# Attention and MLP block on one core: another slot table for the units of two shared PSUM banks, pivot rows copied in their own slot, and scale and shift of the transposed input on ScalarE

## The reference

```python
h = _modulate(_layernorm(x), shift_msa, scale_msa)        # x * (1 + scale) + shift
qkv = h @ W_qkv + b_qkv                                   # 16 heads of 36
scores = jnp.einsum('blhd,bmhd->bhlm', q * scale, k)
attn = jax.nn.softmax(scores, axis=-1)
o = jnp.einsum('bhlm,bmhd->blhd', attn, v).reshape(b, l, c)
x = x + gate_msa * (o @ W_proj + b_proj)
```

## Time and profile before

| what | us |
|---|---|
| median of 3 runs (lowest, highest) | 2611.95 (2607.66, 2615.72) |
| the profiled execution's own time | 2613.1 |
| its span, first to last instruction | 2611.3 |
| PE busy in the span | 2348.9 (90%) |
| DVE busy | 1424.7 (55%) |
| ACT busy | 1100.5 (42%) |
| POOL busy | 807.3 (31%) |
| stretch 130 to 1300 us (attention): PE busy | 1059.1 of 1170.0 |

### The profile page before, as it was taken

The page is one execution under the profiler, slowest core; times in us unless marked ns, Lnnn a source line. Parts: engine busy times, 40 slices in busy tenths (PEclk is TensorE's granted clock), DMA queues, the critical chain, the costliest instruction groups (busy, mean ns, idle before and its releaser), DMA issues. The chain is left out here.

```text
span 2611.3 us, 43520 instructions
## 1 busy us (share of the span) xinstructions
PE 2348.9 (90%) x15081; PEld 2023.5 (77%) x15081; DVE 1424.7 (55%) x2994; ACT 1100.5 (42%) x2362; POOL 807.3 (31%) x1587
## 2 busy tenths in 40 slices
PE   6598989989899898998997269999999999999998
PEld 1466767767677576675775259999999999999998
DVE  3577687777877777777674562333333333333332
ACT  2265555565565565655554122222222222222221
POOL 2044343443544445444444661111111111111110
PEclk9799999999999899999998589999999999999998
DMA  7122222222222222222221340101110101111100
GB/s 233 38 77 71 64 78 74 85 74 64 81 73 81 78 61 79 75 73 87 59 66 49 93 127 12 37 31 37 31 37 31 37 31 37 31 37 31 37 26 28
DMA packets 100228, 159.95 MB, mean 61 GB/s; under 512 B 23680, under 2 KB 44256, under 8 KB 100000
## 3 DMA queue, kind: packets, MB, share of 16 engines
q1 hardware_dynamic: 86752, 110.35, 14.7%
q0 software_dynamic: 12240, 46.60, 5.7%
q10 hardware_dynamic: 1024, 0.26, 0.0%
HBM read 80.10 MB, written 20.16 MB: 38 GB/s over the span
## 5 line engine op out<-in xcount | busy, mean ns | idle before, releaser
L1644 PE MATMUL bank<-h2T,w 128*128 128x256 f32 x4032 | 530.6, 283 | 2.8 <-DVE h2T L1584 2.8
L1644 PEld LDWEIGHTS bank<-h2T,w 128*128 128x128 f32 x4032 | 508.2, 191 | 3.3 <-DVE h2T L1584 3.3
L1553 DVE TENSOR_TENSOR glo<-bank,ghi 128x256 fp32r<-128x256 f32 x288 | 122.1, 424 | 681.3 <-ACT bank L1520 681.3
L1657 PE MATMUL bank<-w,ghi 128*128 128x288 f32 x2304 | 477.3, 298 | 0.0
L1519 ACT ACTIVATE ghi<-bank,b 128x256 fp32r<-128x256 f32 x288 | 136.9, 475 | 680.6 <-PE bank L1644 680.5
L869 DVE TENSOR_TENSOR plo<-pf,phi 128x512 fp32r<-128x512 f32 x512 | 372.4, 727 | 80.0 <-ACT pf L739 77.5
L862 DVE TENSOR_REDUCE negm<-bank 128x1 f32<-128x512 f32 x512 | 347.7, 679 | 77.6 <-PE bank L1018 75.3
L1657 PEld LDWEIGHTS bank<-w,ghi 128*128 128x128 f32 x2304 | 367.1, 189 | 2.1
L1657 PE MATMUL bank<-w,glo 128*128 128x288 f32 x1152 | 340.8, 296 | 0.0
L736 ACT ACTIVATE phi<-bank 128x512 fp32r<-128x512 f32 x512 | 307.3, 600 | 25.8 <-PE bank L1046 11.9
L739 ACT ACTIVATE pf<-bank 128x512 f32<-128x512 f32 x512 | 309.3, 604 | 0.2
(11 more groups left out here) (222 smaller groups left out, 3289.3 us busy)
## 6 DMA issues: line engine op xcount, KB each, us to landing
qs<-qkhi SPq DMA_DIRECT2D x192, 72.0 KB
ks<-qkhi SPq DMA_DIRECT2D x192, 72.0 KB
wst<-w_fc POOLq DMA_DIRECT2D x34, 288.0 KB, 3.1
xln<-x POOLq DMA_DIRECT2D x32, 288.0 KB, 3.5
xln<-x POOLq DMA_DIRECT2D x8, 1152.0 KB, 6.2
x_d<-xln POOLq DMA_DIRECT2D x32, 288.0 KB, 2.5
xa<-x_d SPq DMA_DIRECT2D x32, 288.0 KB, 2.8
xs<-x_d SPq DMA_DIRECT2D x16, 576.0 KB, 3.8
```

The costliest lines, as they stand in the source:

```text
L1644: mm = pe.matmul(F[ft % 2][:, 0:CH], w1[0:rows, w, ft * PAR:(ft + 1) * PAR], h[0:rows, a, :], start=(i == 0), stop=(i == len(FULL_PASSES) ...
L1657: mm = pe.matmul(Y[2 * tt + half][:, 0:HALF], g[ft % 2][:, span], w2[:, ft, w, half * HALF:(half + 1) * HALF], start=(ft == 0 and i == 0), ...
```

## The change

It does four things. `FIRST_SLOT`, `IN_ONE_SLOT` and the slots of statistics, loads and normalisation are other tables. The copy of a pivot row and of an `rv` result (`take_row`, `take_rotation`) is made by DVE in the unit's own slot instead of the next, SP issues the next `wrot` load in the unit's slot instead of two slots later, and `el` h stands in slot 4h+1 for every h, its POOL step in slot 4h+2. `modulate` on DVE is gone: ACT computes `scale * x + shift` twice from the transposed bank, once into `hT` as the high part and once in place in the bank, from which DVE takes the low part as before. The wait for the last low part of `hT`, which tile 0 of `qk` had, goes to whichever unit of the next batch comes first, now `v` 0 0.

```diff
 EARLY_QK = 3
-FIRST_SLOT = [(0, ("v", 1, 0)), (2, ("v", 1, 1)), (4, ("qk", 3)), (6, ("v", 1, 2)), (7, ("tr", 0)), (9, ("p", 0, 0)),
...
+FIRST_SLOT = [(1, ("v", 1, 0)), (3, ("qk", 3)), (6, ("v", 1, 1)), (7, ("tr", 0)), (9, ("qk", 4)), (11, ("p", 0, 0)),
...
-BROADCAST_SLOT = {h: TT * h + 1 for h in range(HEADS)} | {0: 2, 10: 40, 11: 46}
+BROADCAST_SLOT = {h: TT * h + 1 for h in range(HEADS)}
...
-STEP_SLOT = {(38 if _h == 9 else TT * _h + 3): _h for _h in range(HEADS)}
+STEP_SLOT = {BROADCAST_SLOT[_h] + 1: _h for _h in range(HEADS)}
...
                 def hT_his(it, f):
-                    act.wait_ge(modulated, (it + 1) * (KT + 1) + f + 1)
-                    bank = G[g_bank(it, ("ln", f))]
-                    if f < KT:
-                        act.activation(hT[:, f, :], bank[:, :], ACT.Copy).then_inc(hT_hi, 1)
-                    else:
-                        act.activation(hT[0:REM, 2 * KT, :], bank[0:REM, :], ACT.Copy).then_inc(hT_hi, 1)
-                        act.activation(hT[REM:PAR, 2 * KT, :], bank[0:REM, :], ACT.Copy).then_inc(hT_hi, 1)
+                    rows = PAR if f < KT else REM
+                    bank = G[g_bank(it, ("ln", f))][0:rows, :]
+                    grow, add = (adaT[0:rows, j, f, bass.ds(it + 1, 1)] for j in (1, 0))
+                    act.wait_ge(g_full, g_use(it, ("ln", f)) + 1)
+                    for dst in (hT[:, f, :],) if f < KT else (hT[0:REM, 2 * KT, :], hT[REM:PAR, 2 * KT, :]):
+                        act.activation(dst, bank, ACT.Identity, bias=add, scale=grow).then_inc(hT_hi, 1)
+                    act.activation(bank, bank, ACT.Identity, bias=add, scale=grow).then_inc(hT_hi, 1)
...
-                    for u in units(b, ENDS_AT[n]):
-                        if u[0] == "ln":
-                            modulate(b, u[1])
...
+                    for u in units(b, ENDS_AT[n]):
                         if u[0] == "el":
                             take_row(b, u[1], phase)
```

More of the change, by code:

```diff
@@ L81 @@
 EARLY_QK = 3
-FIRST_SLOT = [(0, ("v", 1, 0)), (2, ("v", 1, 1)), (4, ("qk", 3)), (6, ("v", 1, 2)), (7, ("tr", 0)), (9, ("p", 0, 0)),
[5 rows of a table removed]
+FIRST_SLOT = [(1, ("v", 1, 0)), (3, ("qk", 3)), (6, ("v", 1, 1)), (7, ("tr", 0)), (9, ("qk", 4)), (11, ("p", 0, 0)),
[6 rows of a table added]
 RV = 4
-BROADCAST_SLOT = {h: TT * h + 1 for h in range(HEADS)} | {0: 2, 10: 40, 11: 46}
+BROADCAST_SLOT = {h: TT * h + 1 for h in range(HEADS)}
 FIRST_SLOT = sorted(FIRST_SLOT + [(_n, ("el", _h)) for _h, _n in BROADCAST_SLOT.items()], key=lambda at: (at[0], at[1][0] != "el"))
-IN_ONE_SLOT = [("v", 1, 2), ("v", 1, 3), ("p", 0, 1), ("p", 1, 0), ("p", 2, 0), ("p", 2, 1)]
+IN_ONE_SLOT = [("v", 1, 2), ("v", 0, 0), ("v", 0, 1), ("v", 0, 3), ("p", 0, 0), ("p", 0, 1), ("p", 1, 0), ("p", 2, 0), ("p", 2, 1), ("p", 3, 1)]
 TR_SLOT = [_n for _n, _u in FIRST_SLOT if _u[0] == "tr"]
+FIRST_OF_H = [u for _, u in FIRST_SLOT if u[0] == "qk" and u[1] < EARLY_QK or u[0] == "v" and u[1] == 0][0]
 assert all(_n % TT == TT - 1 for _n in TR_SLOT)
 MAX_LEAD = 10
[L95 to L98, removed]
+LOAD_AT = {18: 0, 23: 1, 27: 2, 32: 3}
+STAT_AT = {21: 0, 26: 1, 30: 2, 35: 3}
+INVERT_AT = {31: (0, 3), 36: (3, 4)}
+LN_NORM_AT = {32: 0, 34: 1, 38: 2, 39: 3}
 RESIDUAL_SLOT = 48
 EARLY = 5
-EARLY_SLOT = 28
+EARLY_SLOT = 38
 ACT_LAG, DVE_LAG = 1, 1
-STEP_SLOT = {(38 if _h == 9 else TT * _h + 3): _h for _h in range(HEADS)}
+STEP_SLOT = {BROADCAST_SLOT[_h] + 1: _h for _h in range(HEADS)}
 def shift(unit):
@@ L458, in build @@
         CONSTANTS = RING + 5
-        modulated, hT_hi = sem("modulated"), sem("hT_hi")
+        hT_hi = sem("hT_hi")
         g_full, g_free = sem("g_full"), sem("g_free")
@@ L526, in slot @@
                 def slot(b, n):
-                    for _, i in [u for u in units(b, ENDS_AT.get(n - 2, [])) if u[0] == "rv"]:
+                    for _, i in [u for u in units(b, ENDS_AT[n]) if u[0] == "rv"]:
                         if not isinstance(b, int) or RV * b + i + 1 < RV * BATCH:
@@ L800, in _ @@
                 dve.sem_inc(o_read, 1)
[L802 to L808, removed]
                 def hT_los(it, f):
                     rows = PAR if f < KT else REM
-                    dve.wait_ge(hT_hi, (KT + 2) * (it + 1) + (f + 1 if f < KT else KT + 2))
+                    dve.wait_ge(hT_hi, (2 * KT + 3) * (it + 1) + (2 * f + 2 if f < KT else 2 * KT + 3))
                     part = hT[0:rows, KT + f if f < KT else A_PARTS - 1, :]
@@ L938, in v_tile @@
                     if part == 0:
+                        if u == FIRST_OF_H:
+                            pe.wait_ge(g_free, g_use(it, ("ln", KT)) + 3)
                         pe.wait_ge(g_free, g_use(it, u) + 1)
@@ L948, in qk_tile @@
                     if part == 0:
-                        if t == 0:
+                        if u == FIRST_OF_H:
                             pe.wait_ge(g_free, g_use(it, ("ln", KT)) + 3)
```

## The result

| | before | after |
|---|---|---|
| median of 4 runs | 2612.8 us | 2699.85 us (2696.22 to 2708.07) |
| ratio | 1 | 1.0334, 95% interval 1.0314 to 1.0355 |
| profiled execution (its span) | 2613.1 us (2611.3) | 2696.22 us (2694.4) |
| first to last `values` matmul | 1282.4 us | 1360.4 us |
| one batch, batches 1 to 6 | 164.7 us | 175.0 us |

The changed kernel is 87 us slower, 3.3%. The forecast was slower by 41 us, at 2654, with 2692 as the upper end: the sign is right, the size half of what came. The third stage takes 1205 us in both. All of the loss lies ahead of it: of the 83 us between the two profiled executions, 78 lie in the 512 slots and 5 before the first of them.

The account below looks back on a forecast made before the run. PE was taken to set the attention's pace, busy 1059 of 1170 us. From 2613.1 us, -48 without transfers and +90 for late tiles gave 2655, or 2654 as median; range 2605 to 2692, slower at 0.80.

Parts of the forecast that it names:

- part f: Slots 38 and 54: PE waits about 4.4 us for transfers of late qk tiles, with slower matmuls behind: +90 us.
- the second price: Slots 38 and 54: matmuls behind each transfer wait run at 1.2 GHz, 1.5 us more per wait, 23 us in all.
- The term of 1.5 us: Ahead of the first batch: v 0 0 before qk 0 delays the first tile by 14 matmuls, +1.5 us.
- Part a: Slot 40: pivot row 10 gets four slots after row 9, so PE's wait for POOL shrinks: -30 us.
- Part c: The ln slots: scale and shift on ACT instead of DVE make seven slots together about 1 us shorter: -7 us.
- Parts a to e: All effects except the late tiles' transfers, called the sum without transfers: -48 us.
- part b: Shared banks: 18 units no longer start while the bank they need is being read out: -37 us.
- Part d: Slots 34, 35 and 39: qk 7 and 8 fill short slots where PE waits for DVE's low part: -11 us.
- Part e: Slots behind each tr: the head's transposes wait for DVE to split the bank, without unit work: +37 us.
- The lower clock costs more: Rival: full slots behind the 4.4 us waits cost 2.8 us each, 2675 to 2690; the forecast's upper end.
- The rows arrive in time: Rival at slots 38 and 54: transfers land before PE needs them, so faster, 2565 us; chance 0.14.
- ACT becomes the bound: Rival: ACT sets the pace in the whole stage; chance 0.02, within the forecast's upper end.

Follow-up runs that it names:

- e1_both: The changed kernel with both late tiles moved earlier, qk 7 to slots 31 and 32 and qk 0 to 49 and 50: 2620.05 us, 1.0028.
- e10_row10: The kernel before with scale and shift moved to ACT and pivot row 10 broadcast in slot 41 instead of 40: 2589.25 us, 0.9906.
- e4_before_act: The kernel before, with its own slot table, and only scale and shift moved from DVE to ACT: 2607.60 us, 0.9978.
- e7_dve_mod: The changed kernel with scale and shift moved back to DVE, everything else as changed: 2715.08 us, 1.0393.
- e9_fill: The changed kernel with qk 7 and qk 0 moved earlier, and v 1 2 put in empty slot 24: 2617.69 us, 1.001.
- e6_busy: The changed kernel with unread extra matmuls at slots 9, 17, 21 and 25, written to the next unit's shared bank: 2700.76 us, 1.0336.
- the best table: The kernel before with scale and shift on ACT, pivot row 10 in slot 41, and p 2 0 in slot 22: 2582.98 us, 0.9886.

## Why the prediction was half right

| | forecast | runs | from |
|---|---|---|---|
| late tiles (f) | +90 | +80 | changed kernel less `e1_both` |
| the rest (a to e) | -48 | +6 | `e1_both` less before |
| sum | +42 | +87 | |

The sign came out right because part f, which held, is larger than the rest.

**Part f held.** Place, chain and size: 2.94 and 8.82 us behind V(35) for 3.0 and 9.0. The waits are 3.9 us at slot 38 and 3.1 at slot 54 instead of 4.4, since PE gets there later than at V(35) + 4.6; in the sum that is 8 x 3.9 + 7 x 3.1 = 53 us for 66. The rest of the 80, 27 us, is the second price, put at 23; by the busy times of the changed kernel and `e1_both` it is 31. The first slot starts 5 us later in the profiled execution (V(0) at 129.2 for 123.8); the other kernels lie between 123.9 and 130.0, so that alone can't be told from their spread. The wait ahead of batch 0's first score matmul can: 6.2 us in the changed kernel and in the three runs that keep `v` 0 0 first and add nothing there, 4.3 in the three with tile 0 first, 2.7 on the old table. The term of 1.5 us is right for the order of the two units (1.9); the table adds as much again.

**Part a held.** Slots 40 and 41 take 4.23 us together where they took 7.81, 3.6 a batch for nearly 4. On the old table `e10_row10` gave 18 us for row 10 alone; its slot 40 fell from 4.53 to 1.78 us, 22 us in eight batches, of which slots 41 and 43 took some back.

**Part c held on the old table,** by `e4_before_act` (-6 for -7); on the new one `e7_dve_mod` makes it 15. The duration failed, 0.78 for 0.69 us. The estimate by the figure of the Trainium skill, which made part c about zero, had the duration right and the gain wrong.

**Parts a to e together failed: -48 forecast, +6 measured.** Their account closes from the waits of PE in the two traces. These are the lines of `e1_both`, 130 to 1400 us:

```profile
PE bank L1028 <- ACT pf L741: 33.5, 50, 1.5
PE bank L1052 <- DVE aT L827: 30.3, 28, 2.0
PE bank L1039 <- DVE plo L863: 27.6, 53, 1.0
PE bank L1039 <- ACT ots L748: 10.3, 47, 0.3
PE bank L1012 <- DMA ks<-qklo: 6.4, 10, 2.1
PE bank L1012 <- issue: 3.2, 1, 3.2
```

| standing of PE, 130 to 1400 us | before | `e1_both` | change | forecast |
|---|---|---|---|---|
| pivot rows (a) | 27.9 | 0.6 | -27 | -28 of the -30 |
| banks (b) | 24.0 | 0 | -24 | -24 of the -37 |
| ACT's and DVE's lag: `pf`, `plo`, `hT` (c, d) | 61 | 61 | 0 | -18 |
| transposes behind `tr` (e) | 3.8 | 30.3 | +26 | +37 |
| ACT's copy of the head's output (`ots`) | 0.2 | 10.3 | +10 | none |
| transfers (slots 2 and 54, and one of 3.2 us) | 2.0 | 9.6 | +8 | none |

With 3 us of small ones gone, this is -10 us, as the two stretches say (-9), where the waits in the forecast make -33. The other 15 us of the -48 (2 of part a, 13 of part b) were to come from shorter slots behind the waits, and PE's busy time rose by 12 instead. That is 24 + 27 us, and 3 more stand before the first slot in the profiled executions: together the 54 us between -48 and +6.

**So the steps that failed are these.** *In parts a and b the clock was counted only as a gain.* The waits went as priced, and the low clock of slots 36, 40 to 42 and 48 went too, but `e1_both` has it in slots 9, 17, 45, 46 and 49, and PE is busy 12 us longer in place of 15 shorter. *Part d's and part c's standing was not won*: 61 us in both. Slots 34 and 35 take 1.85 and 2.29 us in `e1_both`, before 1.64 and 2.43. *The emptied slots were priced at nothing*: in slots 8, 16, 20, 24, 40 and 52, which now have no unit, PE works 1.1 to 1.2 us and then stands 0.2 us until ACT has copied the head's output; that is all 10 us of the `ots` line. Slots 5, 29, 42 and 61 of the changed kernel are as short (1.4 us), but PE works all through them. *Part e was sized as a wait and given no clock term*, as the next paragraph shows. Its own four terms also make 5.7 us a batch and not the 5.3 of the text, which is 40 us and not 37.

**Part e held as a wait and failed as a price.** The transposes wait for DVE at slots 9, 17, 21 and 25 of every batch, 28 times, 30.1 us for 3.8 before: +26 for the +37. But behind the wait of 1.66 us at slot 17 the fullest slot of the table runs at 1.2 GHz, and slots 16 and 17 take 8.03 us for 5.33, with less unit work in them than before. The same at slot 49. The timeline of PE in the changed kernel, first a `v` unit at full speed in batch 4, then `v` 0 0 behind its wait in batch 5:

```profile
972.18 2.07 PE L935 MATMUL bank<-wv,hT 128*128 128x288 f32 x14
...
1121.64 0.49 PE L1028 MATMUL bank<-qs,ks 109*128 109x512 f32 x1 [1.45 <-ACT pf L741]
...
1125.22 3.71 PE L935 MATMUL bank<-wv,hT 128*128 128x288 f32 x14
```

It takes 3.71 us for 2.07. Slot 49 takes 5.50 us, before 3.01. Neither slot had a clock term; I asked about the clock only behind waits of over 3 us.

The rows of before could have told this. The prediction takes the 4.14 us of the earlier trace rows for a slot behind a long wait. It is slot 36 of batch 5, the wait ahead of it is of 1.04 us, and its seven matmuls take 2.84 us:

```profile
1026.31 2.84 PE L953 MATMUL bank<-hT,wqk 128*128 128x512 f32 x7
```

The same slot is slow in three batches of the eight (4.1 us) and fast in five (2.6 us), behind waits of the same length. So a low clock behind a short wait was there before the change, in some batches and not in others, and the earlier trace rows show the opposite case, 2.68 us followed by a matmul at 0.50. The Trainium skill (TensorE: Matmul & The Clock Gate, "Why this matters for your kernels") warns of gaps between bursts of matmuls. The trace agrees that gaps go with the low clock, but the gaps here, 1.04 to 1.66 us, are well under the one that the page warns of; the measurement decides.

**The rivals.** "The lower clock costs more" is part of what came, but not where it put it: it had the excess behind the waits of part f, at 2675 to 2690, and it came behind those of part e and of the `ln` slots. "The rows arrive in time" is out by the timeline of slots 38 and 54, "ACT becomes the bound" by 779 of 1364 us. The range ended at 2692 because parts b, d and e were given no bound of their own on the other side; with b and d at nothing, it would have ended at 2740.

**Why the table has these gaps** I can only argue from the code. The count by which a unit knows that its bank is free rises in the order of the table, and a pivot row is now read in its own slot 4h + 1. So a unit of two slots that starts in 4h can't end before the row is read in 4h + 1; the slots 8, 16, 20 and 24, just behind a `tr`, stay empty, and the work moves down until `qk` 7 and `qk` 0 are late. Own-slot reading on the old table was not tried.

## What to carry to other kernels

When a schedule clears conflicts, price what takes their place as carefully as the cleared waits: the new waits of the other engines, and where the low clock goes. And follow each tile to the last transfer that its reader needs. Where PE is the bound, look at the granted clock behind every wait, the short ones too, in all batches and not in one: here waits of 1.04, 1.45 and 1.66 us had slower matmuls behind them in some batches, and it matters most where the slot behind is full. A unit that is moved can also shift a low stretch in slots that were not touched (`e9_fill`, `e6_busy`), so a difference of a few us between two tables says little about the slot that was meant. Compare PE's *busy* time between two traces with the same matmuls: the difference is the clock's share, and here it was half of the loss.

## What the hardware showed that I had not expected

- The granted clock fell to 1.2 GHz behind waits of 1.66 us (slot 17, behind an empty slot that itself had a wait of 0.2), of 1.45 us (slot 48, which has no unit) and, in the kernel before, of 1.04 us (slot 36), and stayed up behind the 2.68 us of the earlier trace rows and behind 1.69 us at slot 17 of batch 1. The length of a wait alone doesn't tell, and what does is not shown here.
- Matmuls whose results nobody reads gave back 42 us of 2700 when they went to a bank that was free, and nothing when they had to wait for theirs. On the best table they still gave 8 us of 2583.
- An activation with two pointer operands takes 781 ns from PSUM to SBUF and 746 ns in place in PSUM. With 64 partitions in place of 128 it is 773 and 727 (same group list as above, ACT, 500 to 1500 us): half the partitions save 1 to 3%.
